# A graph layer's edge loop on VectorE and GpSimd: the waits move behind the address step, and the narrow layers get a ring of eight products

## What is computed

```python
J, HEADS, DIMS = 50, 4, [3, 64, 128, 64]
# 148 edges (i,i+1), (i+1,i), (i,i), sorted
h = (x @ W).reshape(G, Jn, H, C)
e = leaky_relu(es[:, src] + ed[:, dst], 0.2)
alpha = ...                      # softmax of e over the edges that end in one joint
out = zeros(G, Jn, H, C).at[:, dst].add(alpha[..., None] * h[:, src])
x = gelu(layer_norm(out.reshape(G, Jn, H * C) + bias + x @ R, g, b))
```

## Time and profile before

| | |
|---|---|
| median of 3 runs | 6471.19 us (6469.46 to 6471.34) |
| the profiled execution | 6495.84 us |
| its span | 6494.1 us |
| DVE busy | 5697.2 us (88%) |
| GpSimd (POOL) busy | 4760.5 us (73%) |
| ScalarE (ACT) busy | 3243.8 us (50%) |
| TensorE (PE) busy | 3920.4 us (60%) |
| edge loops, first addition to last | 674.8 us for 6 |

### The profile page before, as it was taken

One profiled execution on the slowest core, in us unless ns is written; L12 is line 12 of the kernel. 1 busy time (PEld: TensorE's weight loads), 2 busy tenths in 40 slices (PEclk: granted clock), 3 DMA queues, 4 the chain that ended last, 5 costly groups with the idle time before them and its releaser, 6 DMA issues. The chain is left out here.

```text
span 6494.1 us, 61166 instructions
## 1 busy us (share of the span) xinstructions
PE 3920.4 (60%) x13720; PEld 2254.6 (35%) x13720; DVE 5697.2 (88%) x7312; ACT 3243.8 (50%) x5534; POOL 4760.5 (73%) x3337
## 2 busy tenths in 40 slices
PE   3213412215676776776767767767667676667777
PEld 3102411213343333333433333334333333245556
DVE  3677666765999999999999999999999999967778
ACT  1112211214566656666666666666566665544445
POOL 4362145225999999999999999999999999833334
PEclk9656556657999999999999999999999999987878
DMA  1000000003444444444444444444444444300000
GB/s 26 1 1 11 2 1 1 11 18 116 160 163 168 160 166 165 160 174 160 165 165 160 166 164 161 173 160 165 165 160 166 164 160 170 141 4 2 2 2 2
DMA packets 171496, 695.04 MB, mean 107 GB/s; under 512 B 27970, under 2 KB 34627, under 8 KB 171139
## 3 DMA queue, kind: packets, MB, share of 16 engines
q1 hardware_dynamic: 169608, 688.25, 29.6%
q0 software_dynamic: 1536, 3.14, 0.2%
HBM read 684.77 MB, written 6.55 MB: 106 GB/s over the span
## 5 line engine op out<-in xcount | busy, mean ns | idle before, releaser
L1022 PE MATMUL m_PS<-m_pr,ident 128*128 128x512 f32 (+1 forms) x6144 | 2496.3, 544 | 907.3 <-DVE m_pr L1146 907.1
L806 POOL TENSOR_TENSOR m_hs<-m_u,m_BC 128x1280 f32<-128x1280 f32 x1024 | 2975.9, 2906 | 68.6 <-DVE m_u L1163 68.6
L1138 DVE TENSOR_TENSOR_SCAN m_hs<-m_PS,m_hs 128x640 f32<-128x640 f32 x2048 | 2934.8, 1467 | 5.2 <-POOL m_hs L806 3.0
L863 ACT ACTIVATE m_PS<-m_dt,m_A 128x640 f32<-128x640 f32 x2048 | 1613.3, 794 | 909.9 <-DVE m_hs L1138 896.3
L1022 PEld LDWEIGHTS m_PS<-m_pr,ident 128*128 128x128 f32 x6144 | 1134.9, 195 | 2167.8 <-DVE m_pr L1146 1133.1
L813 POOL TENSOR_TENSOR m_pr<-m_hs,m_BC 128x384 f32<-128x384 f32 x1024 | 1070.1, 1045 | 184.5 <-DVE m_hs L1138 179.9
L1146 DVE TENSOR_TENSOR m_pr<-m_hs,m_PS 128x896 f32<-128x896 f32 x1024 | 1079.8, 1055 | 8.2 <-DVE m_hs L1138 8.0
L270 POOL TENSOR_TENSOR g_prod<-g_hbuf,g_E 128x128 f32<-128x128 f32 (+1 forms) x888 | 471.1, 548 | 832.7 <-ACT g_E L320 636.3
L852 ACT COPY m_PS<-m_BC 128x448 f32<-128x448 f32 x1024 | 546.5, 534 | 155.8 <-DVE m_pr L1146 107.5
L354 PE MATMUL g_TB<-ident,g_nrm 128*128 128x128 f32 x200 | 66.2, 332 | 574.7 <-DVE g_nrm L490 569.9
L557 DVE TENSOR_TENSOR g_accA<-g_accA,g_prod 128x128 f32 x592 | 255.2, 431 | 158.0 <-DVE g_accA L557 122.1
(11 more groups left out here) (241 smaller groups left out, 4435.8 us busy)
## 6 DMA issues: line engine op xcount, KB each, us to landing
m_BC<-m_scr SPq DMA_DIRECT2D x1024, 640.0 KB, 3.8
m_scr<-m_CB SPq DMA_DIRECT2D x32, 160.0 KB, 4.2
m_hs<-in_cwr SPq DMA_DIRECT2D x4, 512.0 KB, 3.9
out<-f_res SPq DMA_DIRECT2D x20, 64.0 KB, 1.5
m_inw<-in_in_w SPq DMA_DIRECT2D x4, 256.0 KB, 4.0
m_dtw<-in_dw SPq DMA_DIRECT2D x4, 256.0 KB, 3.6
m_xw<-in_xw SPq DMA_DIRECT2D x8, 64.0 KB, 3.8
m_outw<-in_ow SPq DMA_DIRECT2D x4, 128.0 KB, 3.4
```

The costliest lines, as they stand in the source:

```text
L806: pool.tensor_tensor(hs[:, g % RH], u[:, p % 2], BC[:, g % UB:g % UB + 1, 0:S].to_broadcast([P, DT, S]), ALU.mult).then_inc(w_ready, 1)
L863: act.activation(half[d], dt_[:, p % 2, d], ACT.Exp, scale=A[:, l, d, n:n + 1]).then_inc(da_ready, 1)
L1022: ins = pe.matmul(Y[:, a:e], ident[:], pr[:, g % RP, a:e], start=False, stop=False, skip_group_check=True)
L1138: v.tensor_tensor_scan(hs[:, g % RH, d, :], half[d], hs[:, g % RH, d, :], 0.0, ALU.mult, ALU.add).then_inc(scan_done, 1)
```

## The change

It does three things in the edge loop and nothing elsewhere.

- The wait of an addition for the addition before it is no longer an instruction ahead of the address step; it is put on the addition itself, which stands behind that step. The wait for the product stays where it was.
- The wait of a product for its place in the ring is likewise put on the product itself.
- The ring is cut by the width of the layer: `SLOTS` is 8, 4, 8. Narrow products then lie one behind the other, 128 elements each, and product e waits for addition e - 8. For the first products of a loop the wait is on all additions of the loop before (`max(..., 0)`).

```diff
+        SLOTS = [RING * P // COUT[l] for l in range(3)]
+
+        def ring_of(l):
+
+            return prod[:].rearrange("p q b c -> p (q b c)").rearrange("p (q b c) -> p q b c", b=2, c=COUT[l])
...
+                        slots = ring_of(l)
                         pool.wait_ge(sm_act, lp * N_SA + N_SA)
                         for e in range(NE):
...
                             j = node(pool, here, src, e)
-                            pool.wait_ge(added, lp * NE + e + 1)
-                            pool.tensor_tensor(
-                                prod[:, e % RING, :, 0:COUT[l]].rearrange("p b (h c) -> p b h c", c=C),
+                            ins = pool.tensor_tensor(
+                                slots[:, e % SLOTS[l]].rearrange("p b (h c) -> p b h c", c=C),
                                 hb[l][:, :, bass.ds(j, 1), :].rearrange("p b o (h c) -> p b (o h) c", c=C),
                                 E[:, :, :, e:e + 1].to_broadcast([P, 2, H, C]),
-                                ALU.mult).then_inc(prod_ready, 1)
+                                ALU.mult)
+                            ins._wait_ge(added, lp * NE + max(e + 1 - SLOTS[l], 0) + RING)
+                            ins.then_inc(prod_ready, 1)
...
                             j = node(v, there, dst, e)
                             v.wait_ge(prod_ready, lp * NE + e + 1)
-                            v.wait_ge(added, lp * NE + e + RING)
                             to = av[:, :, bass.ds(j, 1), :].rearrange("p b o c -> p b (o c)")
-                            v.tensor_tensor(to, to, prod[:, e % RING, :, 0:n], ALU.add).then_inc(added, 1)
+                            ins = v.tensor_tensor(to, to, slots[:, e % SLOTS[l]], ALU.add)
+                            ins._wait_ge(added, lp * NE + e + RING)
+                            ins.then_inc(added, 1)
```

## The result

| | median | ratio to before |
|---|---|---|
| kernel before | 6470.32 us (6468.07 to 6471.34, 4 runs) | 1 |
| changed kernel | 6295.85 us (6291.15 to 6301.10, 4 runs) | 0.9731 (95%: 0.9714 to 0.9748) |

The account below looks back on a forecast made before the run. DVE and GpSimd excluding each other, plus DVE's waits between additions, bounded the edge loops; four narrow passes of 68.2 us and two wide of 118.7 make 510.2 against 674.8, 164.6 less: 6306.6 us, range 6280 to 6378.

Parts of the forecast that it names:

- Split of exclusive and fixed time: Edge loops: only the part growing with elements excludes the other engine; 416 ns per narrow edge, 767 wide.
- The order after a common release: Edge loops, ring full: addition starts at +0.03 us, product at +0.08, so the addition goes first and slow edges vanish.
- Point 1: DVE's addition: wait moved behind its address step; steps fit beside the previous add, chain falls from 502 to 325 ns narrow.
- Loops: Six edge loops: 68.2 us per narrow and 118.7 per wide pass, together 510.2 against 674.8 us.
- the pause: DVE's register load before edge 96 of an edge loop: 5.92 us idle, 5.7 net, stays and no lead hides it.
- The hiccups: Sequencer delays in the edge loops: 1.5 us per narrow pass, bounds 0 and 3.
- Point 4: Ring of eight in narrow loops: no change of pace; seven adds at the end meet no product, 0.6 us per pass.
- Point 2: GpSimd's product: wait moved behind its address step; it starts 0.08 us after the release instead of 0.18.
- Rival 1: Edges behind the pause: the product still wins with a full ring; 636 ns narrow, 987 wide, 6375 us; chance 0.10.
- rival 3: Edge loops: the wait stays ahead of the address step, only the ring acts; 34 us gained, 6437 us; chance 0.04.
- Rival 2 and 4: Edge loops: narrow edges stay at 503 ns, 6358 us, chance 0.08; engines alternate without overlap, 6528 us, chance 0.02.
- the rule that the first holds the pair for the whole instruction: Edge loops: Trainium skill's rule that the first engine fully blocks the other; 661 ns per narrow edge, 6528 us.

Follow-up runs that it names:

- e2: Changed kernel with a ring of four and the addition's wait again ahead of its address step, so only the product's wait is moved: 6426.6 us, ratio 0.9937.
- e8: Kernel before with one superfluous, long-reached wait more per product, so the product starts later: 6384.4 us, ratio to before 0.9821.
- e4: Changed kernel with a ring of four in every layer, both waits still on their instructions: 6295.5 us, ratio to before 0.9733.
- e1: Changed kernel with a ring of four and the product's wait an instruction again, so only the addition's wait is moved: 6303.5 us, ratio 0.9747.
- e7: Kernel before, unchanged, run again for a second profile: 6497.9 us.
- e9: Changed kernel run once more, unchanged, beside e10: 6324.3 us, ratio to before 0.9733.
- e3: Changed kernel with both waits again instructions ahead of the address step, so only the ring is new: 6422.9 us, ratio to before 0.9932.
- e6: Changed kernel with additions reading a fixed piece of PSUM instead of the product, products made but not used: 6232.5 us.
- e5: Changed kernel with ScalarE copying each product to a PSUM bank, from which the addition reads it: 6233.1 us, ratio to before 0.9585.
- e10: Same code as e5, run again beside e9: 6235.3 us, ratio to before 0.9597.

## Why the prediction was right

**Split of exclusive and fixed time: right.** 416 and 767 ns per edge were worked out; the unrounded periods over twelve edges are 417 and 767. The narrow figure is the test: the 65 ns for two handovers in it came from the wide 767 of the kernel before, which the changed kernel only repeats. The 638 and 988 of e2 don't test the split either. They were worked out as the old edge less the product's earlier start, and came out within 2 ns.

**The order after a common release: right, and it is the cause.** +0.03 for the addition and +0.08 us for the product, taken from the statistics and from line 813, came out as 34 and 79 ns. e8 shows that the order alone is worth 108 us; the rest of the 169 is the shorter chain (503 to 417 in narrow edges). Where exactly the tipping point lies between 0.02 behind and 0.035 ahead was not tried.

**Point 1, the steps fit beside the addition: right, narrowly.** Additions that meet no product start 326 ns apart. By the unrounded times of DVE's sequencer the next steps begin 13 to 15 ns after most additions start, and the next address step ends some 235 ns after it; from there to the start it took 47 ns in the kernel before, so 280 in all. Between the address step and the start of an addition that still waits, the sequencer does nothing: in a wide edge it stood from 330.11 to 330.34. The Trainium skill (Perfetto Trace Analysis, DVE / Act Engine Instruction) lets the sequencer go on once the waiting instruction is in the wait queue; this trace doesn't show that. It cost nothing here, as 280 is under 325.

**Loops: 4 us too long, in the small terms.** 68.2 and 118.7 were forecast, 67.7 in the mean and 117.6 measured. By the unrounded starts, edge by edge: in the narrow loops the edges (61.7) and the pause (5.7) are as forecast. The hiccups take 1.1 and not 1.5, and the first two additions behind the pause meet no product and save 0.2. In the wide loops the pause adds 5.4, not 5.7, which was the narrow loops' figure. The 0.4 at the start didn't come; the two additions behind the pause save 0.6; the end saves 0.65 and not 0.9.

**Point 4, the ring: right that it is worth little.** The additions at the end save 0.5 to 0.7 us per narrow loop, 0.6 forecast. Against a ring of four (e4) 0.4 of it per loop was expected to be the ring's; the difference is 0.7 us in all.

**Point 2, the product's wait, was listed as a part of the gain.** It isn't needed: with the old 0.18 against 0.03 the addition is first as well (e1, 1.2 us in the loops).

**Outside the loops** 5.8 us more went than was forecast. The prediction has no term for it. From the end of the last loop to the first scan of Mamba it took 169 us in the shown profile of before and 168 in e7; 162 in changed, e9, e1, e2 and e8; 165 to 166 in e3, e4 and e6; 168 to 170 in e5 and e10. Profiles of one kernel agree within 1.5 us, so it isn't scatter. The traces show TensorE at a different granted clock. Groups of its matmuls in the first Mamba layer, the same 24 before and in the changed kernel (busy us, mean ns):

```profile
L1077 PE MATMUL m_PS<-m_xc,m_dtw 128*128 128x224 f32 (+1 forms) x24 | 10.7, 603 | 3.1 <-ACT m_yz L911 2.7 <-ACT m_CB L903 0.4
L1087 PE MATMUL m_PS<-m_xc,m_dtw 128*128 128x224 f32 (+1 forms) x24 | 6.8, 410 | 3.1 <-ACT m_yz L921 2.7 <-ACT m_CB L913 0.4
```

The granted clock was 0.50 (1.2 GHz) over the first and 0.86 in the mean over the second, that is 2.4 GHz for most of it; the matmuls took 603 and 410 ns, and this stretch ended 4 us sooner. Most of the other 3 us lies in the matmuls of `m_convw` just ahead of it (26.2 and 22.6 us for 64, durations added). In e3, e4 and e6 only these were faster, in e5 and e10 neither. So here the change came with a gain in a stage that it doesn't touch. Why the clock rose when it did stays open, and the runs behind the medians have no trace. Of the 10.8 us by which the forecast was missed 4.1 are the loops', 5.8 lie outside them, and 0.9 is the kernel before, which took 6470.3 and not 6471.2.

**Rivals.** Rival 1 would have held for the product's move alone (e2), rival 3 for the ring alone (e3: 45 us, 34 forecast). Rival 2 and 4 fell with the 417 ns. So did the rule that the first holds the pair for the whole instruction: 661 ns would have been the least.

## What to carry to other kernels

Here two engines that are released by the same event raced for what they share, and some 35 ns decided whether the longer instruction went first; look in the timeline for an instruction that is longer at one place than at another and see who started ahead of it. The better fix was to take the sequencer's steps of the critical engine out from between wait and instruction; delaying the other engine by one step gave two thirds of it. Moving one operand to PSUM with an idle third engine raised the gain by half (262.9 against 173.9 us, e10 and e9). And a gain outside the edited part is worth a look at the granted clock before it is called scatter.

## What was unexpected of the hardware

The set-up ahead of the first loop has two lengths. In the profiles of changed, e1, e2, e3 and e4 the first loop starts at 121.5 to 121.8 us; in the shown profile of before and in those of e5 to e10 at 146.5 to 149.5. In the late ones many short DVE steps of the set-up come 1.4 us apart, with 1.1 to 1.2 us of idle between them, beside GpSimd's indirect DMAs; in the early ones there is no such idle, though the indirect DMAs are 1.30 us apart there too. Timeline of the kernel before, DVE and then GpSimd:

```profile
49.65 0.21 DVE L454 TENSOR_REDUCE g_wc<-g_M 3x4 f32<-3x64 f32 x1 [1.19 <-DVE g_M L453]
51.05 0.21 DVE L453 TENSOR_TENSOR g_M<-g_wc,g_M 3x64 f32<-3x64 f32 x1 [1.19 <-DVE g_wc L454]
52.45 0.21 DVE L454 TENSOR_REDUCE g_wc<-g_M 3x4 f32<-3x64 f32 x1 [1.19 <-DVE g_M L453]
...
49.18 1.00 POOL L250 DMA_INDIRECT x_tok<-in_table,g_ids  x1 [0.30 <-issue]
50.49 0.99 POOL L250 DMA_INDIRECT x_tok<-in_table,g_ids  x1 [0.30 <-issue]
```

The kernel before took 6468 to 6470 us beside the changed kernel and e1 to e4, and 6498 to 6501 beside e5 to e10; its runs within one set lie within 11 us. e1 to e4 ran on one chip and e5 to e10 on another, and the changed kernel started its first loop at 121.5 in the first set and at 146.5 in e9. So it goes with the chip or the session and not with the kernel. It moves the changed kernel's ratio by 0.0002 (0.9731 and 0.9733). What holds the steps back was not looked into.
